# Routed expert layer: from every expert on every token to 272 blocks of 128 sorted rows

## What is computed

```
h      = layernorm(x2) * scale[b] + shift[b]
scores = sigmoid(h @ gate_w.T);  idx = top_k(scores + gate_b, 4)
w      = 2.5 * scores[idx] / sum(scores[idx])
y      = sum over 16 experts of comb[token, e] * (silu(h @ g_e) * (h @ u_e)) @ w2_e
y      = y + (silu(h @ g_s) * (h @ u_s)) @ w2_s         (shared expert)
out    = x2 + gate[b] * y
```

## Time and profile before

| | us |
|---|---|
| median of 3 runs (2477.41 to 2482.58) | 2477.73 |
| the profiled execution | 2475.57 |
| its span, first to last instruction | 2473.8 |
| start of the expert stage in the span | 1242.4 |

### The profile page before, as it was taken

The page is one execution under the profiler, slowest core; times in us unless marked ns, Lnnn a source line. Parts: engine busy times, 40 slices in busy tenths (PEclk is TensorE's granted clock), DMA queues, the critical chain, the costliest instruction groups (busy, mean ns, idle before and its releaser), DMA issues. The chain is left out here.

```text
span 2473.8 us, 41117 instructions
## 1 busy us (share of the span) xinstructions
PE 2236.8 (90%) x13302; PEld 1888.9 (76%) x13302; DVE 1734.5 (70%) x3740; ACT 1043.7 (42%) x1839; POOL 900.1 (36%) x665
## 2 busy tenths in 40 slices
PE   4557999999999999999779999999999999999998
PEld 4546777777777777777568888888888888888887
DVE  5646888888888888888567666666566676666665
ACT  2325555555555555555343333332333332333322
POOL 2421334443344333333333333333333333333333
PEclk7558999999999999999879999999999999999999
DMA  5751111111111111111040000000000000000000
GB/s 203 244 191 58 45 44 44 44 44 43 40 41 38 44 44 39 40 43 36 13 138 28 10 27 27 26 27 18 10 26 26 27 18 10 26 26 27 18 18 9
DMA packets 80253, 116.36 MB, mean 47 GB/s; under 512 B 10992, under 2 KB 44272, under 8 KB 79856
## 3 DMA queue, kind: packets, MB, share of 16 engines
q1 hardware_dynamic: 80112, 114.55, 14.1%
HBM read 71.27 MB, written 43.25 MB: 46 GB/s over the span
## 5 line engine op out<-in xcount | busy, mean ns | idle before, releaser
L1685 POOL TENSOR_TENSOR fl<-ff,fh 128x512 fp32r<-128x512 f32 x272 | 353.5, 1299 | 759.9 <-ACT fh L1479 759.9
L1598 DVE TENSOR_TENSOR ff<-gs,bank 128x512 f32<-128x512 f32 x272 | 186.6, 686 | 379.1 <-ACT gs L1473 325.8
L104 PE MATMUL bank<-mhh,wh 128*128 128x512 f32 x1088 | 435.9, 401 | 9.6 <-issue 9.6
L105 PE MATMUL bank<-mhl,wh 128*128 128x512 f32 x1088 | 431.0, 396 | 0.0
L106 PE MATMUL bank<-mhh,wl 128*128 128x512 f32 x1088 | 430.3, 396 | 0.0
L1620 DVE SCALAR_TENSOR_TENSOR acc<-bank,comb,acc 128x256 f32<-128x256 f32 x960 | 398.0, 477 | 8.8
L1479 ACT ACTIVATE fh<-ff 128x512 fp32r<-128x512 f32 x272 | 172.3, 634 | 446.7 <-DVE ff L1598 413.5
L1473 ACT ACTIVATE gs<-bank 128x512 f32<-128x512 f32 x272 | 162.9, 599 | 367.5 <-PE bank L106 367.5
L104 PE MATMUL bank<-wh,fh 128*128 128x256 f32 x1088 | 306.8, 282 | 3.1 <-POOL fl L1685 1.5
L106 PE MATMUL bank<-wh,fl 128*128 128x256 f32 x1088 | 305.5, 281 | 0.0
L105 PE MATMUL bank<-wl,fh 128*128 128x256 f32 x1088 | 305.3, 281 | 0.0
(11 more groups left out here) (183 smaller groups left out, 4571.9 us busy)
## 6 DMA issues: line engine op xcount, KB each, us to landing
px<-in_x SPq DMA_DIRECT2D x16, 512.0 KB, 5.0
h_t<-phT SPq DMA_DIRECT2D x16, 512.0 KB, 5.1
h_hi<-phh SPq DMA_DIRECT2D x16, 512.0 KB, 5.8
h_lo<-phl SPq DMA_DIRECT2D x16, 512.0 KB, 4.9
hTh<-h_hi SPq DMA_DIRECT2D x32, 256.0 KB, 2.7
hTl<-h_lo SPq DMA_DIRECT2D x32, 256.0 KB, 2.9
hT<-h_t SPq DMA_DIRECT2D x32, 256.0 KB, 2.6
xr<-in_x SPq DMA_DIRECT2D x32, 256.0 KB, 2.6
```

The costliest lines, as they stand in the source:

```text
L104: pe.matmul(out, a_hi, b_hi, start=start, stop=False, skip_group_check=True)
L105: pe.matmul(out, a_hi, b_lo, start=False, stop=False, skip_group_check=True)
L1598: dve.tensor_tensor(ff[e % 2][:, :], g, UP[e % 2][:, :], ALU.mult).then_inc(ff_done, 1)
L1685: pool.tensor_tensor(fl[e % 2][:, :], ff[e % 2][:, :], fh[e % 2][:, :].bitcast(F32), ALU.subtract).then_inc(fl_done, 1)
```

## The change

`experts` is replaced by four functions, with a barrier of all engines behind each.

`route` walks over the 16 groups. It normalises, makes the logits, chooses 4 experts, and counts by matmuls with triangular and all-one matrices how many tokens before this one chose the same expert. From that follows for each token and choice a row in `xs_dram`, where each expert has room for all tokens (`CAP` rows). The modulated tokens are turned back to rows on PE, and POOL scatters them: 16 indirect transfers of 128 rows of 1 KB for each group. The shared expert is computed here for all tokens, and x2 plus its gated result goes to `x2s_dram`. The weights are loaded and split here too, one expert for each group.

`plan` rounds each expert's count up to 128, sums, and makes a table with 272 blocks (256 full ones of routed rows, and one for each expert's rounding): the first row of each block and its expert's column in the weights. POOL clears 128 rows behind each expert's last one.

`blocks` walks over 136 pairs of blocks. For each pair SP reads two numbers of the table into registers and loads 2 x 128 rows. PE turns them (4 transposes), makes gate and up with the tokens stationary and 256 weight columns moving (12 matmuls, at a register address), turns the product (2 transposes) and makes down (6 matmuls, at a register address). ACT copies the result out of PSUM, and SP stores it. All buffers are double. POOL meanwhile works out the rows to gather.

`combine` walks over 64 tiles of 128 tokens. POOL gathers 4 rows for each token (256 indirect transfers in all, 4 tiles ahead), ACT and DVE weight and add them, and add `x2s_dram`.

The core of the diff (`+` lines are the new functions'; the whole body of the old `experts` goes):

```diff
-        experts(nc, sem, prime, t, mod, gate_b_row, ident, minus_half, bank, x2_dram, out)
+        experts(nc, sem, t, mod, gate_b_row, ident, minus_half, bank, x2_dram, x2s_dram, xs_dram, ys_dram, out)
...
+EW = KD * 2 * INTER + D
+CAP = SEQ * NB + P
+ROWS = NE * CAP + NE * P
+TILES = NB * SEQ // P
+BLOCKS = NB * SEQ * TOPK // P + NE
+PAIRS = BLOCKS // 2
...
+        route(nc, sem, t, mod, gate_b_row, ident, minus_half, bank, wh, wl, dest, weight, run,
+              x2_dram, x2s_dram, xs_dram)
+        plan(nc, sem, t, ident, bank, run[0], table, shift, xs_dram)
+        blocks(nc, sem, ident, bank, wh, wl, table, dest, shift, source, xs_dram, ys_dram)
+        combine(nc, sem, gate_b_row, source, weight, x2s_dram, ys_dram, out)
...
+                for n in range(GROUPS):
+                    logits(n)
+                    turn_back(n)
+                    up(n)
+                    if n + 1 < GROUPS:
+                        turn(n + 1)
+                    positions(n)
+                    down(n)
...
+                def apply(n):
+                    dve.wait_ge(root, n + 1)
+                    if n > 0:
+                        dve.wait_ge(xT_ps, KD * n)
+                    for c in range(MT):
+                        last = dve.tensor_scalar(xn[:, c, :], x2[n % XBUF][:, c, :], mv[n % 2][:, c, 0:1],
+                                                 rs[n % 2][:, c:c + 1], ALU.subtract, ALU.mult)
+                    last.then_inc(xn_done, 1)
...
+                for n in range(GROUPS):
+                    if n + 1 < GROUPS:
+                        norm(n + 1)
+                    low(n)
+                    choose(n)
+                    if n + 1 < GROUPS:
+                        apply(n + 1)
+                    weigh(n)
+                    times(n)
+                    assign(n)
+                    lo(n)
+                    weights_lo(n + 1)
+                    with_shared(n)
...
+            def _(pool):
+                def invert(n):
+                    pool.wait_ge(eps, n + 1)
+                    pool.tensor_tensor(rs[n % 2][:, :], rs[n % 2][:, :], minus_half[:, :], ALU.pow).then_inc(root, 1)
+                def scatter(n):
+                    pool.wait_ge(dest_done, n + 1)
+                    pool.wait_ge(rows_done, 2 * (n + 1))
+                    for c in range(MT):
+                        for k in range(TOPK):
+                            pool.indirect_dma_start(
+                                out=xs_dram[:, :],
+                                out_offset=bass.IndirectOffsetOnAxis(ap=dest[:, n * MT + c, k:k + 1], axis=0),
+                                in_=rows[n % 2][:, c, :], in_offset=None).then_inc(scattered[n % 2], 16)
+                invert(0)
+                for n in range(GROUPS):
+                    if n + 1 < GROUPS:
+                        invert(n + 1)
+                    scatter(n)
+                for n in range(2):
...
+                for e in range(NE):
+                    pool.indirect_dma_start(out=xs_dram[:, :],
+                                            out_offset=bass.IndirectOffsetOnAxis(ap=pad_at[:, e:e + 1], axis=0),
+                                            in_=zero[:, :], in_offset=None).then_inc(cleared, 16)
+                pool.wait_ge(cleared, 16 * NE)
...
+                def load(u, par):
+                    rows = [at(u, n) for n in range(2)]
+                    if from_(u, 2):
+                        sp.wait_ge(xT_ps, u - 1)
+                    for n in range(2):
+                        sp.dma_start(x[par][:, n, :], xs_dram[bass.ds(rows[n], P), :]).then_inc(x_in[par], 16)
+                def store(u, par):
+                    sp.wait_ge(yo_done, u + 1)
+                    sp.dma_start(ys_dram[bass.ds(u, 1)].rearrange("o n p d -> p (o n) d"), yo[par][:, :, :]
+                                 ).then_inc(y_out[par], 16)
+                def step(u, i, par, last=False):
+                    if not last:
+                        load(u + 2, par)
+                    if from_(u, 1):
+                        store(u - 1, 1 - par)
...
+                def at(u, n):
+                    return pe.value_load(table[0:1, 1, bass.ds(2 * u + n, 1)], min_val=0, max_val=(NE - 1) * EW)
+                def turn(i, par):
+                    pe.wait_ge(x_in[par], 32 * (i + 1))
+                    for k in range(KD):
+                        for n in range(2):
+                            last = pe.transpose(XT[par][:, (k * 2 + n) * P:(k * 2 + n + 1) * P],
+                                                x[par][:, n, k * P:(k + 1) * P], ident[:, :])
+                    last.then_inc(xT_ps, 1)
...
+                def down(u, par):
+                    bases = [at(u, n) for n in range(2)]
+                    pe.wait_ge(fh_done, u + 1)
+                    pe.wait_ge(fl_done, u + 1)
+                    if from_(u, 2):
+                        pe.wait_ge(yo_done, u - 1)
+                    for n in range(2):
+                        cols = bass.ds(bases[n] + KD * 2 * INTER, D)
+                        last = split3(pe, DN[par][:, n * D:(n + 1) * D], fh[par][:, n, :], fl[par][:, n, :],
+                                      whf[:, cols], wlf[:, cols], n == 0, n == 1)
+                    last.then_inc(down_ps, 1)
+                def step(u, i, par, last=False):
+                    up(u, 0, par)
+                    if from_(u, 1):
+                        turn_f(u - 1, 1 - par)
+                    up(u, 1, par)
+                    if not last:
+                        turn(i + 1, par)
+                    if from_(u, 1):
+                        down(u - 1, 1 - par)
...
+                def take_y(u, i, par):
+                    act.wait_ge(down_ps, u + 1)
+                    if from_(u, 2):
+                        act.wait_ge(y_out[par], 16 * i)
+                    act.activation(yo[par][:, :, :].rearrange("p n d -> p (n d)"), DN[par][:, :], ACT.Copy
+                                   ).then_inc(yo_done, 1)
+                def step(u, i, par, last=False):
+                    if from_(u, 1):
+                        split_f(u - 1, 1 - par)
+                    silu_gate(u, par)
+                    if not last:
+                        split_x(u + 2, par)
+                    if from_(u, 1):
+                        take_y(u - 1, i - 1 + par, 1 - par)
+                split_x(0, 0)
...
+                for n in range(TILES):
+                    if n >= YBUF:
+                        pool.wait_ge(used, n - YBUF + 1)
+                    for k in range(TOPK):
+                        pool.indirect_dma_start(out=y[n % YBUF][:, k, :], out_offset=None, in_=ys_dram.rearrange("u n p d -> (u n p) d"),
+                                                in_offset=bass.IndirectOffsetOnAxis(ap=source[:, n * TOPK + k:n * TOPK + k + 1], axis=0)
+                                                ).then_inc(y_in[n % YBUF], 16)
...
+                    dve.wait_ge(y_in[n % YBUF], 16 * TOPK * (n // YBUF + 1))
+                    for k in range(1, TOPK):
+                        ins = dve.scalar_tensor_tensor(a, y[n % YBUF][:, k, :], weight[:, n, k:k + 1], a,
+                                                       ALU.mult, ALU.add)
+                        if k == TOPK - 1:
+                            ins.then_inc(used, 1)
+                            dve.wait_ge(used, n + 1)
+                        else:
+                            then_wait(ins)
+                    then_wait(dve.tensor_tensor(a, a, gate_b_row[g // MSTEPS][:, :], ALU.mult))
+                    if c == 0:
```

More of the change, by code:

```diff
@@ L1323, in experts @@
+        stored = [sem(f"r_stored{n}") for n in range(2)]
+        loads = [(gatew, "gate_w"), (gateb, "gate_b"), (earlier, "earlier"), (ones, "ones"), (slot0, "slot0")]
+        ORDER = [NE] + list(range(NE))
         with nc.Block() as block:
@@ new lines, in _ @@
+                load(0)
+                for tile, name in loads:
+                    sp.dma_start(tile[tuple(slice(None) for _ in tile.shape)], t[name]).then_inc(consts, 16)
+                load_weights(0)
+                load(1)
+                load_weights(1)
+                for n in range(GROUPS):
+                    if n + 2 < GROUPS:
+                        load(n + 2)
+                    if n + 2 <= NE:
+                        load_weights(n + 2)
+                    store(n)
+                for n in range(2):
+                    sp.wait_ge(stored[n], 16 * GROUPS // 2)
@@ L1418, in down @@
+                def down(n):
+                    pe.wait_ge(fh_done, n + 1)
+                    pe.wait_ge(fl_done, n + 1)
                     for c in range(MT):
@@ L1425, in down @@
                         if c % 2 == 1:
                             last.then_inc(down_ps, 1)
-                def group(n, b, j, first=False, last=False):
-                    for e in range(ALL):
-                        up(e, n, b, first)
-                        if e > 0:
```

(47 more changed lines are left out.)

906 lines of the change are left out of this document (563 added, 343 removed).

## The result

The changed kernel takes 3359.78 us (median of 4 runs, 3354.08 to 3360.82) against 2477.57 before: a ratio of 1.355, 95% interval [1.353, 1.357]. The profiled execution took 3354.08 us with a span of 3352.3. I had predicted 3130, so the direction is right, and 223 us of span are missing from the sum.

The account below looks back on a forecast made before the run. PE was taken to bound the old expert stage, at full clock. The forecast summed 1242.4 unchanged + 437 route + 28 plan + 1095 blocks + 315 combine + 12 barriers = 3129 us span, predicted 3130 us, 26% slower; range 2750 to 3560.

Parts of the forecast that it names:

- What takes PE's place: In each of the four new stages, the loop of waits closing once per turn was to set the pace instead of PE.
- Rival 1: In `blocks`, loads run ahead and PE alone sets the pace: 2.76 us a pair, 389 us, 2425 us in all; chance 0.03.
- `blocks`, 1095: 136 turns of 7.95 us through SP's store and the next load, plus 14 us to fill and drain; bounds 774 to 1775.
- nine register operations: In `blocks` on SP, between store and next load: with two table reads they were to take 1.13 us.
- the forecast's own case: Turns of 7.2 to 8.8 us in `blocks` and indirect transfers of 0.9 to 1.6 us each; chance 0.45.
- Rival 2: In `blocks`, table reads are slow, 0.8 us: the turn is 9.55 us, the time 3350 us; chance 0.2.
- The floor of a tensor load: In `blocks`, about 600 ns under each table read would add 0.8 us a turn, 109 us in all, giving 3240.
- The clock in `blocks`: The profile after was to show a granted clock of 0.5 in `blocks`.
- `route`, 437: First destinations at 26 us, 15 turns of 26.0 us, each 16 indirect transfers at 1.2 plus 6.8; bounds 370 to 821.
- The starvation rule: GpSimd's transfers starve for descriptors while DVE runs in a two-port mode, so each takes longer in `route` than in `combine`.
- `combine`, 315: 256 gathers at 1.2 us are 307, with first landing and last tile 315 us; bounds 194 to 699.
- DVE 186 us; hidden: In `combine`, DVE's five chained operations and handovers take 2.9 us per tile, 186 us, hidden.

Follow-up runs that it names:

- store_on_act: Changed kernel with the blocks' result store moved from SP's queue to ACT's, right behind the copy; 2850.53 us, ratio 1.151.
- invert_mid: Changed kernel with GpSimd computing group n+2's square root in the middle of group n's scatters in `route`; 3285.90 us, ratio 1.326.
- gather_2: Changed kernel with `combine` gathering two of each token's four rows and using each twice; span 3174.7 us, the stage 188 us.
- by_group: three_edits with DVE's and ACT's part of `combine` done for four tiles at once and eight gather buffers instead of four; 2687.06 us, ratio 1.084.
- three_edits: Changed kernel with store_on_act, invert_mid and one table read less per turn on PE; 2693.53 us, ratio 1.087.
- four_edits: three_edits with the accumulator of `combine` in PSUM instead of SBUF; 2692.32 us, ratio 1.086.

## Why the prediction came out as it did

- **What takes PE's place.** Right: a loop of one load per pair through SP's store in `blocks`, GpSimd in the other two. `store_on_act` shows the loop by cutting it, 504 us at once. In `route` DVE waits 9.3 us a group for the power, where I had put 4 to 6. Rival 1's price for a PE without that loop, 389 us, was also wrong: with the loop cut `blocks` takes 735, since 2.76 a pair left out four table reads.
- **`blocks`, 1095 against 1237.** The mechanism was right and terms were mis-sized. From the store's issue to the next load it takes 2.32 us on the mean, not 1.53. Of this the store's issue is 0.41 and the two reads are 0.77, as predicted with 0.4 and 0.8. The step that failed is "nine register operations", 0.33 us by the 0.037 of the earlier trace rows: what stands beside the reads takes 1.14, namely 0.15 for the operation behind each read, about 0.05 for the others, the gaps between them, and the loop's branch in every second turn. From the transposes to `down` it is 1.68, not 1.1, by the same cause. The loads were over-sized, 2.64 from the first one's issue where I had 3.02. Together the turn is 9.16 in place of 7.95, 165 us over 136 turns. Start and end took back some 22: the first three turns, with all buffers free, take 2 to 4 us.
- **A hit near a rival's number.** The turn lies outside the forecast's own case, 7.2 to 8.8 us. Rival 2's time, 3350 us, is the nearest of all, and that is luck: its reads of 0.8 us each are 0.38 and 0.30, its turn of 9.55 us is too long, and its `route` and `combine` are 93 us too short.
- **The floor of a tensor load.** The Trainium skill's figure of about 600 ns (DMA: Bandwidth & Descriptors, section on latency and other measured facts) is not borne out for the instruction: its record is 0.30 us on PE and 0.27 to 0.54 on SP, 0.597 at the longest. What a read with its arithmetic takes from the loop is 0.52 us on PE and 0.83 on SP.
- **The clock in `blocks`.** Right for the steps of the loop: in the turn shown, `down`'s matmuls start 0.21 us apart, which is the 1.2 GHz of the earlier trace rows. The stage's mean granted clock is 0.64, so other parts of it ran at 2.4 GHz. That cutting the loop would give the full clock back I had not said; in `store_on_act` it is 0.98.
- **`route`, 437 against 477.** A scatter with its gap is 1.32 (1.02 and 0.30), not 1.2: 2 us of a turn. The rest of the turn is about 7.5, not 6.8. The step that failed is that I followed DVE through `weigh` and `times`, while PE's eight transposes and the positions, at half clock, end 1.93 us later. `invert_mid` took that chain off the path.
- **The starvation rule.** A scatter takes 1018 ns on the mean and a gather 974, so g is a little longer in `route`. That agrees in sign with the Trainium skill (SBUF — State Buffer, section on who interferes with whom), but it is 11 us over 256 scatters and no starvation, and a scatter is not a gather. Like with like, a gather takes 1043 ns in `gather_2`, where DVE is busier, 974 in the changed kernel and 946 with the accumulator in PSUM. How much of `route`'s difference is DVE's is not shown.
- **`combine`, 315 against 368.** A gather is 1.27, not 1.2: 19 us. The step that failed is "DVE 186 us; hidden": its chain has late waits that bring it to 6.9 us a tile in stretches, GpSimd waits 30 us for buffers that it has not freed, and what follows the last gather is some 5 us longer than my 8. `by_group`, with fewer waits and more buffers, has neither; which of the two did it is open. The cause of the late waits isn't settled: straight code or loops, SBUF or PSUM, wide or narrow rows made no difference to the time. Only with half of the gathers, where DVE nearly always has its data, were they rare. One fact is unexplained too: in all kernels with 256 gathers and four buffers the first and the last gather start 352 to 355 us apart, whether 21 or 48 tiles are late.
- **Sum of the misses.** 40 - 1 + 142 + 53 - 12 = 222 of the 223 us.
- **Why nothing beats the kernel before.** The best version, `by_group`, is 8.4% slower. GpSimd's 512 transfers of rows at about 1.3 us are 660 us, over half of the 1231 that the old stage took, and in this order of stages nothing of the blocks lies beside them. With the rest of `by_group` as it is, `blocks` would have to end in 440 us, and it takes 650 with PE still waiting for its own reads.

## What to carry to other kernels

Before work is left out on the bound engine, count what chooses it: here 128 rows moved by an indirect transfer cost 1.27 to 1.32 us of GpSimd, and a table read with its arithmetic about 0.5 to 0.8 us of a sequencer. Look at the spread of such a read and not at its median alone. Draw the loop of waits through the queue that issues both loads and stores. A store that waits for this turn's result must not stand ahead of the next turn's load; on ACT's queue, right behind the copy that it waits for, its issue did not lengthen the turn, and the move gave 15% of the time. In this loop TensorE idled and its mean granted clock was 0.64; with the loop cut it was 0.98, so cutting it gave more than the idle time.

## What the runs showed of the hardware that was not expected

- The register operation right behind a read from SBUF took 0.15 us, on SP and on PE; the others beside it took about 0.05. This held for all 272 reads on SP and all 544 on PE.
- A read of the table on SP took 0.27 us where no store stood ahead of it in the queue (`store_on_act`). In the changed kernel one of the two reads behind each store's issue took 0.46 or 0.54 us. Why is open.
- Indirect transfers of 128 rows cost the same for 256 bytes a row as for 1024: the 256 gathers were busy 250.3 and 249.3 us.
- The same gathers took 946 ns instead of 974 when VectorE's accumulator beside them lay in PSUM, and 982 and 946 in `three_edits` and `four_edits`.
- Waits of VectorE for its own previous instruction mostly ended on steps of 0.70 us in stretches of the combining stage, up to 3.4 us late, while its instructions kept their length. With loops in place of straight code they came in bursts. The cause is open.
